# Three LayerNorms kept feature-major in a convolution, attention and mixture-of-experts block

## The reference

```python
x = x + conv(group_norm(x))       # info 16 x mask 16 products, then 1x1 to 64 channels, relu
t = tokens(x)                     # (32, 1024, 64)
t = t + attn(layernorm(t))        # linear attention, 8 heads
t = t + ffn(layernorm(t))         # 8 experts, top 2
def attn(x):                      # x is normalised: LayerNorm 1
    Q, K = elu(x @ Wq) + 1, elu(x @ Wk) + 1
    msg = (Q @ KV) * Z @ Wm
    msg = layernorm(msg) * g1 + b1                 # LayerNorm 2
    h = relu(concat([x, msg]) @ W1) @ W2
    return x + layernorm(h) * g2 + b2              # LayerNorm 3
def ffn(x):                       # x is normalised: LayerNorm 4
    out = sum(gate[e] * (gelu(x @ W1[e] + b1[e], exact) @ W2[e] + b2[e]) for e in range(8))
```

## Time and profile before

| | |
|---|---|
| median of 3 runs | 1180.87 us (1180.21 to 1181.57) |
| profiled execution | 1182.04 us, its span 1180.2 us |
| PE busy | 1080.6 us, 92% of the span |
| DVE, ACT, POOL busy | 790.7, 682.4, 363.3 us |
| mean granted PE clock | 0.987 |
| one turn in the steady part | 139.8 and 140.5 us in turn |

### The profile page before, as it was taken

The page is one execution under the profiler, slowest core; times in us unless marked ns, Lnnn a source line. Parts: engine busy times, 40 slices in busy tenths (PEclk is TensorE's granted clock), DMA queues, the critical chain, the costliest instruction groups (busy, mean ns, idle before and its releaser), DMA issues.

```text
span 1180.2 us, 15496 instructions
## 1 busy us (share of the span) xinstructions
PE 1080.6 (92%) x5878; PEld 487.5 (41%) x5878; DVE 790.7 (67%) x1673; ACT 682.4 (58%) x930; POOL 363.3 (31%) x277
## 2 busy tenths in 40 slices
PE   3798689989999899998999999998999989999898
PEld 1463445423544246342464335442354424634232
DVE  5675836696658876587674976669665887656534
ACT  2256365665765546765656656656566555676454
POOL 0010032243313423234312433224331343324465
PEclk9999989999999999999999999999999999999999
DMA  4010097008610195003920068100861019300580
GB/s 150 1 35 3 1 216 146 19 1 199 146 36 19 30 224 126 1 19 81 225 73 1 19 144 199 36 19 0 189 156 36 19 38 226 81 1 19 120 203 21
DMA packets 17418, 96.64 MB, mean 82 GB/s; under 512 B 3648, under 2 KB 6720, under 8 KB 13120
## 3 DMA queue, kind: packets, MB, share of 16 engines
q1 hardware_dynamic: 17344, 95.66, 34.9%
HBM read 77.82 MB, written 9.44 MB: 74 GB/s over the span
## 4 chain that ended last, share of the span: by engine, by line
PE 65%; DVE 18%; ACT 12%; issue 4%; SPq 1%; DMA 0%; DVEq 0%; POOL 0%; POOLq 0%; ACTq 0%
PE HP L809 13%; PE HP L823 10%; PE R L658 6%; PE R L614 5%; PE R L745 5%; PE R L603 4%; ACT H L957 4%; PE R L594 4%; DVE SM L1141 3%; PE R L752 2%; PE R L676 2%; PE R L667 2%; DVE TM L1290 2%; PE R L823 2%; DVE SM L1057 2%
## 5 line engine op out<-in xcount | busy, mean ns | idle before, releaser
L1002 POOL TENSOR_TENSOR XB<-TM,XB 128x512 f32<-128x512 f32 x254 | 325.2, 1298 | 663.4 <-DVE TM L1290 663.4
L957 ACT ACTIVATE H<-HP,W 128x1024 f32<-128x1024 f32 x224 | 240.5, 1113 | 129.8 <-PE HP L809 129.2
L809 PE MATMUL HP<-XF,W1E 64*128 64x512 f32 x1024 | 267.9, 631 | 20.0 <-DVE TM L1290 19.6
L823 PE MATMUL HP<-H,W 128*64 128x512 f32 x896 | 232.3, 614 | 24.4 <-ACT H L957 24.4
L1290 DVE SCALAR_TENSOR_TENSOR TM<-HP,B2S,CWB 128x512 f32<-128x512 f32 x224 | 161.3, 744 | 57.1 <-PE HP L823 56.2
L1141 DVE TENSOR_REDUCE SM<-T 128x8 f32<-128x512 f32 x128 | 84.3, 681 | 109.3 <-ACT T L892 108.1
L809 PEld LDWEIGHTS HP<-XF,W1E 64*128 64x128 f32 x1024 | 84.6, 186 | 150.0 <-DVE TM L1290 84.5
L892 ACT ACTIVATE T<-R 128x512 f32<-128x512 f32 x128 | 75.2, 604 | 83.5 <-PE R L658 77.3
L823 PEld LDWEIGHTS HP<-H,W 128*64 128x64 f32 x896 | 46.7, 135 | 172.3 <-ACT H L957 135.6
L1113 DVE SCALAR_TENSOR_TENSOR BIG<-R,T 128x512 f32<-128x512 f32 x112 | 69.6, 681 | 26.8 <-PE R L594 26.6
L614 PE MATMUL R<-W,T 128*128 128x128 f32 x512 | 73.2, 283 | 7.1 <-DVE T L1160 5.6
(11 more groups left out here) (165 smaller groups left out, 1371.0 us busy)
## 6 DMA issues: line engine op xcount, KB each, us to landing
CWB<-gates_hbm SPq DMA_DIRECT2D x32, 1536.0 KB, 21.9
CWB<-gates_hbm SPq DMA_DIRECT2D x32, 512.0 KB, 10.0
BIG<-XN SPq DMA_DIRECT2D x32, 256.0 KB, 4.5
out<-XB SPq DMA_DIRECT2D x15, 512.0 KB, 3.0
X<-x SPq DMA_DIRECT2D x14, 512.0 KB, 7.2
W<-wpack SPq DMA_DIRECT2D x1, 1064.0 KB, 5.0
XF<-x SPq DMA_DIRECT2D x2, 512.0 KB, 6.2
gates_hbm<-CWR SPq DMA_DIRECT2D x16, 64.0 KB, 1.6
```

The source lines that it names most:

```text
L809: last = mm(HP[u % BATCH][:, half(k)], W1E[img(k), e, :], XF[img(k), 1 - par, s, half(c)], start=True, stop=True)
L823: last = mm(sums_of(b, u)[img(k), :], w("w2e")[:, C * e:C * e + C], activated(b, u)[:, k, :], start=True, stop=True)
L957: f(activated(b, u).rearrange("p k t -> p (k t)"), HP[u % BATCH][:, :], ACT.Gelu, bias=col(B1E + e))\
L1002: nc.gpsimd.tensor_tensor(acc, TM[:, u % BATCH, :], acc, ALU.add).then_inc(acc_done, 1)
```

## The change

1. LayerNorm 2, 3 and 4 stay feature-major. The mean is taken out by one matmul per piece with the centring weights (`by_feature`; for 3 it is already in W2C). ACT squares into T2 (`centred`) and copies the centred values to T1 (`kept`). `variance` on PE sums the squares over the features with 16 matmuls of 128 tokens each, stationary operand 128x32 (`LINES`), the four pieces on four column tiles, into one 128x128 block in R[1]. `root` on DVE makes the inverse root in 9 steps on 128x128. `spread` on PE gives it to all features with 16 matmuls of 128 tokens, stationary 32x128 (`SPAN`), the four pieces on four row tiles. `scaled` on DVE multiplies PSUM by T1. LayerNorm 3 has one more DVE step (bias and residual from XB). The transposes of line 614, the sums of line 1141 for k = 2 to 4 and `message_norm` are gone.
2. The MLP input needs no U: `hidden` is two K=64 matmuls per image and piece, one on XN with W1X, one on T1 with W1G, into one accumulation. The DMA from XN is gone. The second write of `features_1` (XB with bias) is gone; POOL forms XB from XN and X and takes over the wait on `out_done`.
3. `prepare` moves behind `low_1.0` in `OPENING`; the wait for it is now at `conv_out` (and at `group_stats` of the early group). It needs six more small DMAs (`w1_in`); eight more bring SPAN. They stand in SP's queue behind those of SPREAD.
4. `CWR` lies in a part of RT, so the wait on `cw_out` moves from `gate_rows` to `choose_1`. `group_norm` waits for `h_ps` instead of `u_in`.
5. `SCHEDULE` and `OPENING` are other lists.

```diff
 SCHEDULE = [
...
+    ("channel_stats", "HH", 1, 0), ("gates", "", 1, 0), ("gate_tokens", "YY", 0, 0),
+    ("gate_exp", "", 0, 2), ("group_stats", "H", 0, 0), ("group_norm", "HYY", 2, 2),
+    ("choose_1", "", 0, 0), ("info_mask_0", "HHY", 0, 2), ("choose_2", "YH", 3, 1),
+    ("info_mask_1", "HYY", 1, 1), ("gate_rows", "HH", 2, 0), ("info_0.1", "", 0, 1),
+    ("info_0.0", "YY", 1, 1), ("low_0.1", "", 0, 0), ("low_0.0", "HH", 1, 0), ("high_0.1", "", 0, 0),
+    ("high_0.0", "YY", 0, 2), ("info_1.1", "", 0, 0), ("info_1.0", "HH", 1, 0), ("low_1.1", "", 1, 0),
+    ("low_1.0", "YY", 0, 2), ("high_1.1", "", 0, 0), ("high_1.0", "HH", 2, 0), ("conv_out.1", "YY", 0, 2),
+    ("conv_out.0", "", 0, 0), ("centre_1.1", "", 0, 0), ("first_unit", "", 0, 0), ("finish_1", "", 0, 0),
+    ("centre_1.0", "", 1, 0), ("rstd_1", "HH", 0, 0), ("norm_1.0", "", 1, 1), ("norm_1.1", "Y", 0, 2),
+    ("weights_1", "Y", 0, 0), ("features_1.0", "H", 0, 0), ("features_1.1", "H", 2, 0),
+    ("query.1", "", 0, 0), ("query.0", "YYH", 0, 0), ("key.1", "", 0, 0), ("key.0", "", 0, 1),
+    ("finish_0", "", 1, 0), ("key_value.1", "", 0, 0), ("key_value.0", "", 0, 0), ("kv_turn.1", "Y", 0, 0),
+    ("kv_turn.0", "", 0, 0), ("kv_values.1", "", 0, 0), ("kv_values.0", "", 0, 0),
+    ("denominator", "", 0, 1), ("numerator.0", "", 0, 0), ("numerator.1", "H", 2, 0),
+    ("attended.0", "", 0, 0), ("attended.1", "H", 0, 0), ("message.1", "", 0, 0), ("message.0", "Y", 0, 1),
+    ("variance_2", "HY", 0, 0), ("rstd_2", "Y", 1, 0), ("spread_2", "", 1, 2), ("norm_2.0", "HH", 1, 0),
+    ("hidden_0.0", "", 0, 0), ("norm_2.1", "", 0, 0), ("hidden_0.1", "", 0, 1), ("hidden_1.0", "", 0, 0),
+    ("hidden_1.1", "Y", 0, 0), ("hidden_out.1", "", 0, 0), ("hidden_out.0", "YH", 0, 0),
+    ("variance_3", "", 0, 1), ("rstd_3", "HYY", 3, 1), ("spread_3", "", 1, 1), ("norm_3.0", "HH", 0, 0),
+    ("centre_4.0", "", 0, 0), ("norm_3.1", "Y", 0, 0), ("centre_4.1", "YH", 0, 0),
+    ("variance_4", "HYY", 0, 2), ("rstd_4", "", 1, 2), ("spread_4", "", 0, 0), ("norm_4.0", "", 0, 0),
+    ("norm_4.1", "", 1, 0),
 ]
...
+                def variance(k):
...
+                    for s in range(G):
+                        pe.wait_ge(ln_sq[s], at(a * LNS + k, LAST))
+                    pe.wait_ge(cp_done, copies(k) + 1)
+                    for q in range(NQ):
+                        lines = LINES[:, 2 * (NQ - 1 - q):2 * (NQ - 1 - q) + 32]
+                        for i, (s, c) in enumerate(PIECES):
+                            last = mm(R[G - 1][32 * i:32 * i + 32, CH:CH + P], lines, T2[:, s, some_tokens(c, q)],
+                                      start=(q == 0), stop=(q == NQ - 1))
+                    last.then_inc(var_ps, 1)
+
+                def spread(k):
...
+                    pe.wait_ge(rs_done, a * (LNS - 1) + k - 1)
+                    pe.wait_ge(cp_done, copies(k) + len(PIECES))
+                    for q in range(NQ):
+                        for i, (s, c) in enumerate(PIECES):
+                            rows = slice(32 * i, 32 * i + 32)
+                            last = mm(R[s][:, some_tokens(c, q)], SPAN[rows, q, :], ROOTS[rows, 3, :], start=True, stop=True)
...
-                        mm(R[s][:, half(c)], W1G[:, :], U[s][k][:, half(c)], start=True, stop=True)\
-                            .then_inc(h_ps[s], 1)
...
+                        for k in range(2):
+                            mm(R[s][:, half(k)], W1X[img(k), :], XN[img(k), s, half(c)], start=True, stop=False)
+                        for k in range(2):
+                            mm(R[s][:, half(k)], W1G[img(k), :], T1[img(k), s, half(c)], start=False, stop=True)\
+                                .then_inc(h_ps[s], 1)
...
+                def centred(k, slots):
+
                     for s, c in pieces(slots):
                         act.wait_ge(ln_ps[s], at(a * LNS + k, c))
                         f(T2[:, s, half(c)], R[s][:, half(c)], ACT.Square).then_inc(ln_sq[s], 1)
+                        if (s, c) == PIECES[-1]:
+                            kept(k, s, c)
+
+                def kept(k, s, c):
+
+                    f(T1[:, s, half(c)], R[s][:, half(c)], ACT.Copy, scale=col(G2) if k == 3 else 1.0).then_inc(cp_done, 1)
+
+                def variance(k):
+                    for s, c in PIECES[:-1]:
+                        kept(k, s, c)
...
+                def root(k):
+
+                    dve.wait_ge(var_ps, a * (LNS - 1) + k - 1)
+                    h, g, t, y = (ROOTS[:, i, :] for i in range(4))
+                    link(v.tensor_scalar(h, R[G - 1][:, CH:CH + P], 0.5 * LN_EPS, None, ALU.add))
...
+                def scaled(k, s, c, dst):
+
+                    dve.wait_ge(ln_back[s], at(a * LNS + k, c))
+                    return v.scalar_tensor_tensor(out=dst, in0=R[s][:, half(c)], scalar=ROOT_SCALE, in1=T1[:, s, half(c)],
+                                                  op0=ALU.mult, op1=ALU.mult)
...
+                def scale_hidden(s):
+                    for c in range(NCH):
+                        scaled(3, s, c, T1[:, s, half(c)]).then_inc(y3_done[s], 1)
+                    dve.wait_ge(xs_done[s], a + 1)
+                    for c in range(NCH):
+                        dve.wait_ge(y3_done[s], at(a + 1, c))
+                        v.scalar_tensor_tensor(out=XB[:, par, s, half(c)], in0=T1[:, s, half(c)], scalar=col(B2),
+                                               in1=XB[:, par, s, half(c)], op0=ALU.add, op1=ALU.add)\
+                            .then_inc(x2_done[s], 1)
```

More of the change, by code:

```diff
@@ L49 @@
 NW_FIRST = COLS["ow"][0]
+NW_HELD = COLS["fold"][0]
 B_IM, B_OUT, G1, B1, G2, B2, B1E, B2E = 0, 1, 2, 3, 4, 5, 8, 16
@@ L55 @@
 NORMS = 2 * TB
+NQ = CH // P
+ROOT_SCALE = 3.375
 FAR = 1e30
@@ L90 @@
 OPENING = [
-    "channel_stats", "group_stats", "group_norm", "prepare", "info_mask_0", "info_mask_1",
[12 rows of a table removed]
-    "gates", "gate_tokens", "gate_exp", "next centre_1.0", "choose_1", "choose_2", "next centre_1.1",
-    "gate_rows", "next rstd_1", "next norm_1.1", "next features_1.1", "next norm_1.0", "next features_1.0",
-    "weights_1",
[15 rows of a table added]
 ]
@@ L753, in hidden_out @@
                                       start=True, stop=True)
[L754 to L759 removed]
+                        last.then_inc(ln_ps[s], 1)
                 def centre_4(slots):
@@ L935, in numerator, with hidden @@
                         f(T1[:, s, half(c)], R[s][:, half(c)], ACT.Copy).then_inc(num_done[s], 1)
-                def hidden(k, slots):
-                    for s, c in pieces(slots):
-                        act.wait_ge(h_ps[s], at(a * 2 + k + 1, c))
-                        f(HA[s][k][:, half(c)], R[s][:, half(c)], ACT.Relu, bias=BH[:, :]).then_inc(h_done[s], 1)
+                def hidden(c, slots):
+                    for s in slots:
+                        for k in range(2):
+                            act.wait_ge(h_ps[s], at(a * 2 + c + 1, k))
+                            f(HA[s][k][:, half(c)], R[s][:, half(k)], ACT.Relu, bias=BH[:, :]).then_inc(h_done[s], 1)
                 def gates():
```

189 lines of the change are left out of this document (98 added, 91 removed), and 48 rows, old and new, of tables (OPENING, SCHEDULE).

## The result

The changed kernel takes 1175.5 us (median of 6 runs, 1173.1 to 1178.4) against 1181.2 before: ratio 0.995, interval [0.9937, 0.9963]. That is 5.7 us faster. The prediction said 1166.0, faster by 15. Its direction and range held, its size did not. The profiled execution took 1173.5 us, its span is 1171.7 against 1180.2.

What follows compares the result with a forecast made beforehand. PE's queue was taken to bound the kernel: 1182.0 profiled, less 13.3 for seven turns and 2.1 for the opening, gives 1166.6, as a median 1165.4, stated as 1166. The range was 1145 to 1190, the forecast's own 1158 to 1177.

Steps and rivals of the forecast that it cites:

- the clock of the turns: Router stretch of the turn: a clock mean of 0.94 was read there, and no term was made of it.
- Sum -2.1: Opening: -4.6 for the earlier info_mask, +1.0 for `prepare`, +1.5, -1.1 and +1.1 for norms 2, 3 and 4.
- the walk: New instruction lists followed with assumed durations: the turn's four stretches at 22.4, 26.4, 27.2 and 62.2 us.
- the step from the profiled execution to the median: Whole kernel: the median was put 1.2 us below the profiled time, 1165.4 from 1166.6.
- Sum 138.2: Forecast length of one turn in us, the sum of its four stretches.
- -1.9 per turn: Steady turns: 138.2 against 140.1 us, times seven turns -13.3 us.
- Its first term: Opening: info_mask on PE starts at 11.4 instead of 16.0 us because `prepare` moves, -4.6 us.
- A: Rival: small tiled matmuls, mainly `spread`, run slower than their columns; 1187 us, or 1229 with `variance` slow too; chance 0.20.
- C: Rival: mode changes by `variance`, `spread` and K=64 `hidden` cost 12.6 us in all; 1178 to 1180 us; chance 0.13.
- the 1.0 that the sum took for V and S: PE in norms 2 to 4: `variance` and `spread` 1.0 us each, priced by columns; three of each 6.0 per turn.
- B: Rival: a quarter of the turn's 12 us of PE waits goes, another -3 a turn; 1145 us; chance 0.25.
- The sharing with POOL: `root` on DVE slows while POOL adds: at worst 13 us over seven turns, at best 0; 0 in the sum.

Runs made afterwards that it cites:

- e7: Changed kernel with the two `gate_rows` transposes issued six times in each turn, filling PE's wait in the router: 1169.3 us.
- e13: The kernel of e7 run again, unchanged, in another series: 1172.0 us.
- e6: Changed kernel with `gates`, `gate_tokens` and `gate_exp` of the opening put back ahead of the early group's centre_1 and rstd_1: 1175.0 us.
- e14: The kernel of e12 with the opening's first transfer of gate weights to CWB cut in two, expert 0 by itself: 1168.7 us.
- e10: The kernel of e7 with `prepare` put back in front of info_mask_0: 1182.4 us.
- e12: The kernel of e7 with PE's waits in the opening and the tail's router also filled, by 10 and 2 matmuls: 1168.6 us.
- e15: The kernel of e12 with all fills, run once more for comparison on the same chip as e14: 1169.6 us.
- e5: Changed kernel with the 16 matmuls of each `spread` issued twice: 1191.9 us.
- e1: Kernel before with only `prepare` moved, from the front of the opening to behind high_0.1: 1179.6 us.
- e9: Kernel before with ten 128-column matmuls put on PE in the router of each turn from the third on: 1183.8 us.

## Why the size was wrong

The sum was 1165.4 and 1175.5 was measured. No single term makes the difference. Three were mis-sized: the clock of the turns, which the prediction put at nothing though it had read 0.94 (2.4 us in this profile); the opening, "Sum -2.1", which came out as 0.0 because work and a transfer stood in the path where the walk had none; and the step from the profiled execution to the median.

**The turn: right, with a reference that was too high.** "Sum 138.2" is what five of the six turns between the marks take, and the stretches are 21.8, 26.5, 26.7 and 63.2 where the walk had 22.4, 26.4, 27.2 and 62.2. Errors of -0.6, +0.1, -0.5 and +1.0 cancel, so that the sum is right to 0.0 is partly luck; `hidden`, 0.7 us shorter than the 7.7 put in, is as much as the first. But "against 140.1" took the two turns of the earlier trace rows for a pattern. The longer kind is a turn with a fall of the clock, two in six; the mean is 139.9 (839.36 / 6), and most turns without a fall take 139.5. So -1.9 per turn is -1.7 on the mean and -1.3 at equal clock.

**A clock that falls: a term put at nothing.** The prediction read 0.94 in the earlier trace rows and made no term of it. Behind a wait of 1.2 to 1.5 us in the router PE may run at half clock, at 1.0 to 2.4 us a time (in the turn of the earlier trace rows, 1.0). The change left the wait in place. The profile of after has one such turn (+2.4); filling the wait, in e7 and e13, took all falls of the turns away, and the median is 3.2 us lower. Six turns: -11.4 forecast, +1.2 for the reference, +2.4 for the fall, which is the measured -7.7 to 0.1.

**The opening: the step whose path was wrong.** "Sum -2.1" came out as 0.0. Its first term shows in the trace: info_mask is 3.8 us earlier, message_0 4.5. At the first `hidden` 0.9 is left (96.11 against 97.05): `message` takes 6.2 us from its start instead of 3.8, as in this execution its first half ran at the lower clock (3.6 us for four instructions, the other half 1.9) and a replicate stands between the halves, and the chain of norm 2 is longer by the rest. At centre_4 it is 2.8 again (119.41 against 122.20). From there to the gates the changed kernel takes 17.6 us instead of 11.6. Three things make the 6.0: centre_4 takes 5.6 instead of 3.8, since its second slot waits 1.7 for the extra XB step of LayerNorm 3, which the walk priced in the turn and the sum of the opening doesn't name; the fourth norm takes 2.1 more, not 1.1; and the early group's centre_1 in front of the gates, which the sum does not have, adds 2.1 (1.8 of it is gone in e6). The gate rows are 2.6 later than before. Then, where before 13.6 us lay between the gate rows and the first combine (145.7 to 159.2), 10.9 are left, and the transfer of the gate weights, which those 13.6 covered, now ends last (e14 shows it). The combine comes at 159.2 in both kernels. I had walked PE, DVE and ACT through the opening but not the DMA that starts at its end.

**The rest.** The seventh turn's share was to be -1.9; the time from the last mark to the end is -0.8 at equal work, where the tail's router has a fall of the clock that the tail of before has not. In e10, e12, e14 and e15, whose tails have none, it is 152.7, 2.0 less than before at equal work: the term was right without the fall. The profiled run is 2.0 us below the median, where I had it 1.2 above. Together: +3.7 in the six turns, +2.1 in the opening, +1.1 behind the last mark and +3.2 between profile and median are the 10.1 us by which 1175.5 lies above the 1165.4 of the prediction's sum. The 3.2 come from the scatter of 5 us between runs, for which the falls (e7) and the opening (e13, e15) were shown as sources, not in what proportion.

**Rivals.** A, slow tiled matmuls, fell: V 1.02, S 1.10. C, changes of mode, is not there either. The Trainium skill (TensorEngine Tiling (Array Packing), Key Properties) has each change of mode drain TensorE. The runs show a price that agrees with it: an S right behind another S takes 0.9 (e5), one between groups of other modes 1.10, so the changes of mode at its ends cost 0.2 us together at most. But the 1.0 that the sum took for V and S already held 0.15 for them, from line 702, and V and S lie only 0.02 and 0.10 above it. `hidden`, which C also counted, came out 0.7 below its term. So C's further 12.6 us are not there. B, more from the waits, went the other way: PE's idle time grew by 1.4 and 2.1 us a turn. The sharing with POOL is real but hits little of `root`: of the 24 executions of its second step, seven stood beside an addition of POOL and took 892 to 900 ns, the others 226 to 229, and no two-input step of `root` met one. One line of DVE in the changed kernel, shortest, median, longest:

```profile
L1199 DVE TENSOR_SCALAR BIG<-BIG x24: 226/227/900, 91.0 to 1059.4; 128x128 int32<-128x128 int32 x24
```

The root that meets an addition takes 3.4 us and not 2.7, and S waits 0.15 for it. The Trainium skill (GPSIMD Engine Reference, 1. Specifications) says that POOL and DVE contend for two SBUF inputs and for DVE's 2-port mode; line 1199 has one input, so by that rule it would be the mode, which no run here separates.

**Open.** Why message_0 starts anywhere from 80.5 to 84.0 us in the changed opening; why `prepare` in front costs 8 to 11 us there (e10) and 1.4 to 3 in the old one (e1); why the same wait in the router is followed by a fall of the clock in some turns and not in others; and in what proportion the falls and the opening make the scatter of the runs.

## What to carry to other kernels

Take the turn without falls of the clock as the reference, and count a wait like that of 1.2 to 1.5 us here twice: as a wait, and as the half clock that may follow. Filling it with PE work of about its length (e7, e13) removed the falls and gave the lower median, and too long a fill (e9) cost more than it gave. When the opening gets shorter on the engines, walk the transfers that it starts as well, since one that was covered becomes the next wait. A feature-major norm is cheap here only where its crossings between engines are covered: in the old order, not tuned for it, the same instructions cost 95 us more.

## What the runs showed of the hardware

- 32 instructions of 128 columns on four column tiles take 1.02 us, on four row tiles 1.10; a second group of the latter right behind takes 0.9.
- Two K=64 matmuls of 512 columns on different row halves, accumulating with two more, take 0.86 us; one K=128 matmul of 512 columns takes 0.87.
- The same DVE step, an int32 TENSOR_SCALAR of 128x128 with one input, takes 226 ns alone and 900 beside an addition of POOL (after, line 1199).
- The store of the gate weights landed in 1.2 us in twelve of the seventeen profiles and in 3.0 to 3.3 in five, and in none between.
- A kernel with 1.5 us more matmul work per turn had a median 3.2 us lower; in all seven profiles with that work PE stayed at 2.4 GHz in the turns, in none of the seven without it.
